# A decoder block on one core: the attention product of the folded weights in three float32r passes instead of one float32 product

## The reference

```python
x = _layernorm(x + _L0_attn_ref(x, ...))      # eight heads of eight columns
x = _layernorm(x + _L0_xattn_ref(ctx, ctx, x))
x = _layernorm(x + _L0_ffn_ref(x, ...))       # linear layer plus a chosen low-rank part
x = _layernorm(x + _L1_attn_ref(x, ...))      # codes looked up, see below
x = _layernorm(x + _L1_xattn_ref(x, ctx, ...))
x = _layernorm(x + _L1_ffn_ref(x, ...))       # ternary weights
```

```python
q, k, v = (_lin_lora(x, _dequant(codes[n], scales[n]), A[n], B[n]) for n in (0, 1, 2))
attn = (q + k + v) / 3.0
o = _lin_lora(attn, _dequant(codes[3], scales[3]), A[3], B[3])
x1 = x + o
h = silu(_lin_lora(x1, gate)) * _lin_lora(x1, up)
return x1 + _lin_lora(h, down)
```

## Time and profile before

| what | us |
|---|---|
| median of 3 runs (lowest, highest) | 634.55 (633.81, 635.37) |
| the profiled execution's own time | 634.79 |
| its span in the trace | 633.0 |
| PE busy in the span | 620.7 |
| DVE busy | 449.5 |
| ACT busy | 388.7 |
| POOL busy | 64.7 |

### The profile page before, as it was taken

How to read it: one execution, slowest core, us unless ns; L and a number is a source line. 1 busy time by engine, 2 the same in 40 slices (tenths; PEclk the granted TensorE clock), 3 DMA queues, 4 the chain that set the end, 5 groups by cost and what they waited for, 6 DMA issues and landing times.

```text
span 633.0 us, 8684 instructions
## 1 busy us (share of the span) xinstructions
PE 620.7 (98%) x3186; PEld 460.6 (73%) x3186; DVE 449.5 (71%) x718; ACT 388.7 (61%) x564; POOL 64.7 (10%) x116
## 2 busy tenths in 40 slices
PE   9999999999999999999999999999999999999996
PEld 6655555544568888878888888887777788887874
DVE  5788787557678979898987627334675777777467
ACT  2977798746677688686966136232558545667532
POOL 1032133211130000000000000001221000000012
PEclk9999999999999999999999999999999999999999
DMA  8763486302134135443630005019001133200002
GB/s 254 286 186 114 163 277 208 101 1 86 56 91 119 51 98 153 131 141 91 180 108 19 1 0 167 1 50 419 30 1 34 50 101 100 67 0 2 1 34 101
DMA packets 25777, 64.46 MB, mean 102 GB/s; under 512 B 5601, under 2 KB 10785, under 8 KB 24966
## 3 DMA queue, kind: packets, MB, share of 16 engines
q1 hardware_dynamic: 23478, 62.19, 30.6%
q10 hardware_dynamic: 2256, 1.70, 0.9%
HBM read 59.27 MB, written 4.60 MB: 101 GB/s over the span
## 4 chain that ended last, share of the span: by engine, by line
PE 80%; ACT 7%; DVE 5%; DMA 4%; issue 2%; SPq 1%; POOL 0%; POOLq 0%; DVEq 0%; ACTq 0%
PE bank L1126 19%; PE bank L1262 10%; PE bank L1114 5%; PE bank L1115 5%; PE bank L1113 5%; PE bank L965 4%; PE bank L885 4%; PE bank L689 3%; ACT line L1398 3%; DMA b_gu<-in_b_gu 2%; PE bank L995 2%; PE bank L824 2%; PE bank L1204 2%; PE bank L1205 2%; DMA codes<-in_c_qkv 1%
## 5 line engine op out<-in xcount | busy, mean ns | idle before, releaser
L1398 ACT ACTIVATE line<-line 128x1024 f32<-128x1024 f32 x87 | 91.4, 1050 | 0.1
L1113 PE MATMUL bank<-xh,wh 128*128 128x512 f32 x224 | 87.4, 390 | 0.0
L1114 PE MATMUL bank<-xl,wh 128*128 128x512 f32 x224 | 87.4, 390 | 0.0
L1115 PE MATMUL bank<-xh,wl 128*128 128x512 f32 x224 | 87.3, 390 | 0.0
L1126 PE MATMUL bank<-wh,xh 128*128 128x512 f32 x176 | 69.7, 396 | 0.2 <-DVE xl L2387 0.2
L1126 PE MATMUL bank<-wh,xl 128*128 128x512 f32 x176 | 68.6, 390 | 0.0
L2387 DVE TENSOR_TENSOR xl<-arena,xh 128x1024 fp32r<-128x1024 f32 (+1 forms) x24 | 28.3, 1179 | 35.7 <-ACT xh L1703 35.5
L1703 ACT ACTIVATE xh<-arena 128x1024 fp32r<-128x1024 f32 (+1 forms) x24 | 24.4, 1021 | 39.6 <-PE bank L1126 35.3
L1115 PEld LDWEIGHTS bank<-xh,wl 128*128 128x128 f32 x224 | 42.0, 188 | 8.8
L1113 PEld LDWEIGHTS bank<-xh,wh 128*128 128x128 f32 x224 | 42.1, 188 | 8.6
L1114 PEld LDWEIGHTS bank<-xl,wh 128*128 128x128 f32 x224 | 42.1, 188 | 8.4
(11 more groups left out here) (288 smaller groups left out, 1354.2 us busy)
## 6 DMA issues: line engine op xcount, KB each, us to landing
codes<-in_c_gu SPq DMA_DIRECT2D x14, 512.0 KB, 5.1
scales<-in_s_gu SPq DMA_DIRECT2D x28, 256.0 KB, 3.9
codes<-in_t_gu SPq DMA_DIRECT2D x8, 512.0 KB, 4.3
codes<-in_c_dn SPq DMA_DIRECT2D x7, 512.0 KB, 5.0
scales<-in_s_dn SPq DMA_DIRECT2D x14, 256.0 KB, 3.9
fold<-in_t_dn SPq DMA_DIRECT2D x1, 3584.0 KB, 15.7
codes<-in_c_qkv SPq DMA_DIRECT2D x6, 512.0 KB, 4.6
scales<-in_t_gu SPq DMA_DIRECT2D x6, 512.0 KB, 4.1
```

Of the source, the lines that this page charges most:

```text
L1113: pe.matmul(dst, wh[:, s, c:c + P], xh[:, k, cols], start=(k == 0), stop=False)
L1114: pe.matmul(dst, wh[:, s, c:c + P], xl[:, k, cols], start=False, stop=False)
L1115: last = pe.matmul(dst, wl[:, s, c:c + P], xh[:, k, cols], start=False, stop=(k == KD - 1))
L1398: nc.scalar.activation(below(slot), below(slot), ACT.Prelu, bias=bias, scale=scale, alpha=alpha).then_inc(bent, 1)
```

## The change

`attention_product` multiplies in three float32r passes. For that, ACT makes high parts of the four parts of `wsum` and of `woT` (`rows_high(j)`, two copies of 128 x 512 in each of the steps 0 to 3), and DVE subtracts them in place to get the low parts (`rows_low(j)`, two instructions in each of the same steps). One semaphore, `af_added`, counts all six instructions of a j. The high parts lie in `fold` and in `wh`. The high part of the down stack, which lay in `wh`, now lies in `m_hi`, so it is made and used up earlier: `down_stack_hi` moves from steps 2 and 3 to 0 and 1, `down_stack_low` from step 4 to 1, and the other two stacks move back, to steps 2 and 3 on ACT and to 5 and 6 on DVE. The units of the lookup, one in each step before, stand as 1, 0, 1, 0, 2, 1, 2, 1.

```diff
-PLAN = ([0] + [1] * (NT - 1), [2], [0] + [1] * 7, [1] * NT)
+PLAN = ([0] + [1] * (NT - 1), [2], [0] + [1] * 7, [1, 0, 1, 0, 2, 1, 2, 1])
...
-        ad_high = wh[:, :, :].rearrange("p s c -> p (s c)")[:, 0:FF]
+        ad_high = m_hi[:, :, :].rearrange("p k c -> p (k c)")[:, 0:FF]
+        w_hi = [fold_r[:, NF - 6 + n, :] for n in range(KD)]
+        wo_hi = [wh[:, n // 2, n % 2 * D:(n % 2 + 1) * D] for n in range(KD)]
+        w_lo, wo_lo = (arena_r[:, m_at:m_at + KD * D].rearrange("p (j c) -> p j c", j=KD) for m_at in (0, KD * D))
...
                 if n >= 2 and not o:
-                    pe.wait_ge(af_added, n)
+                    pe.wait_ge(af_added, 3 * n - 4)
...
                 if c == 0:
-                    pe.wait_ge(af_added, 2 * KD)
+                    pe.wait_ge(af_added, 6 * KD)
...
                 for j in range(KD):
-                    pe.matmul(dst[:, :], wsum[:, j, c * P:(c + 1) * P], woT[:, j, :], start=(j == 0), stop=False)
+                    pe.matmul(dst[:, :], w_hi[j][:, cols], wo_hi[j], start=(j == 0), stop=False)
+                    pe.matmul(dst[:, :], w_hi[j][:, cols], wo_lo[:, j, :], start=False, stop=False)
+                    pe.matmul(dst[:, :], w_lo[:, j, cols], wo_hi[j], start=False, stop=False)
                 pe.matmul(dst[:, c * P:(c + 1) * P], threes, ident[:, :], start=False, stop=True).then_inc(m_ps, 1)
...
+            def rows_high(j):
+
+                act.wait_ge(af_added, 6 * j + 2)
+                if j == 0:
+                    act.wait_ge(kq_ps, NT)
+                nc.scalar.activation(w_hi[j], wsum[:, j, :], ACT.Copy).then_inc(af_added, 1)
+                nc.scalar.activation(wo_hi[j], woT[:, j, :], ACT.Copy).then_inc(af_added, 1)
...
                 act.wait_ge(m_ps, c + 1)
+                if c == 0:
+                    act.wait_ge(stack_low, 1)
...
                 for u, h in half_plan(3, t, 0):
                     unit_bends(u, h)
+                if t < KD:
+                    rows_high(t)
                 if t >= 1:
                     norm_tail(2 * NT + t - 1)
                 if FIRST_M <= t < FIRST_M + KD:
                     m_high_of(t - FIRST_M)
+                if t == 0:
+                    act.wait_ge(in_lora, 16 * 4)
+                if t < 2:
+                    down_stack_hi(t)
+                elif t < 4:
+                    stack_hi_of(t - 2)
...
-                if t < 2:
-                    stack_hi_of(t)
-                elif t < 4:
-                    down_stack_hi(t - 2)
...
+            def rows_low(j):
+
+                dve.wait_ge(af_added, 6 * j + 4)
+                nc.vector.tensor_tensor(w_lo[:, j, :], wsum[:, j, :], f32(w_hi[j]), ALU.subtract).then_inc(af_added, 1)
+                nc.vector.tensor_tensor(wo_lo[:, j, :], woT[:, j, :], f32(wo_hi[j]), ALU.subtract).then_inc(af_added, 1)
...
-                if t in (1, 2):
-                    stack_low_of(t - 1)
+                if t in (NT - 3, NT - 2):
+                    stack_low_of(t - NT + 3)
                 for u, h in half_plan(3, t, 0):
                     unit_part(u, h)
-                if t == 4:
+                if t == 1:
                     down_stack_low()
+                if t < KD:
+                    rows_low(t)
```

More of the change, by code:

```diff
@@ L217, in decoder_kernel @@
         m_hi = sb("m_hi", [P, KD, D], F32R)
+        with nc.sbuf_tensor("fold_r", [P, NF, D], F32R) as fold_r:
+            pass
         fold = sb("fold", [P, NF, D])
@@ L993, in attention_product @@
                 dst = bank[4 + c % 2]
+                cols = slice(c * P, (c + 1) * P)
                 for j in range(KD):
-                    pe.matmul(dst[:, :], wsum[:, j, c * P:(c + 1) * P], woT[:, j, :], start=(j == 0), stop=False)
+                    pe.matmul(dst[:, :], w_hi[j][:, cols], wo_hi[j], start=(j == 0), stop=False)
+                    pe.matmul(dst[:, :], w_hi[j][:, cols], wo_lo[:, j, :], start=False, stop=False)
+                    pe.matmul(dst[:, :], w_lo[:, j, cols], wo_hi[j], start=False, stop=False)
                 pe.matmul(dst[:, c * P:(c + 1) * P], threes, ident[:, :], start=False, stop=True).then_inc(m_ps, 1)
@@ L2221, in add_lora @@
                 nc.vector.tensor_tensor(dst, dst, bank[4 + n % 2][:, :], ALU.add).then_inc(af_added, 1)
+            def rows_low(j):
+                dve.wait_ge(af_added, 6 * j + 4)
+                nc.vector.tensor_tensor(w_lo[:, j, :], wsum[:, j, :], f32(w_hi[j]), ALU.subtract).then_inc(af_added, 1)
+                nc.vector.tensor_tensor(wo_lo[:, j, :], woT[:, j, :], f32(wo_hi[j]), ALU.subtract).then_inc(af_added, 1)
             def stack_low_of(part):
-                dve.wait_ge(stack_hi, part + 1)
+                dve.wait_ge(stack_hi, part + 3)
                 if part == 0:
@@ L2231, in down_stack_low @@
             def down_stack_low():
-                dve.wait_ge(stack_hi, 4)
+                dve.wait_ge(stack_hi, 1)
                 nc.vector.tensor_tensor(ad_st[2 * RG:STACK, :], a_down[2 * RG:STACK, :], f32(ad_high[2 * RG:STACK, :]), ALU.subtract).then_inc(stack_low, 1)
```

## The result

The changed kernel takes **636.86 us** (median of 7 runs, 636.46 to 637.73), and the kernel before, on the same chip, 635.37 (7 runs, 633.81 to 635.77). The ratio is 1.0024, with a 95% interval of 1.0014 to 1.0034: slower by 1.5 us, within 0.3%, as forecast. The forecast had 0.6 us. The median before was 0.8 us higher in this comparison than the 634.55 on which the forecast was built, so of the 1.7 us between 635.2 and 636.86 some 0.8 belongs to the baseline and 0.9 to the forecast of the change.

What follows compares the result with a forecast made beforehand. PE, busy for 98% of the span, was taken to bound the kernel. A gain of 2.52 us and waits of 1.14, 1.0 and 1.0 gave +0.6 us on 634.55, so 635.2 us as median, range 632.5 to 637.2.

Steps and rivals of the forecast that it cites:

- my own case: Whole run: PE's saving less three waits, +0.6 us, 635.2 us as median, own range 633.9 to 636.4, chance 0.52.
- The gain: PE in `attention_product`: twelve float32r matmuls take 2.80 us instead of 3.43, so four products save 2.52 us.
- First wait: `ffn_W(4)` in step 2: PE waits for DVE's add of `ln_head(1)` to empty its bank, losing 1.14 us.
- Second wait: `attention_product(0)` in step 3: PE waits for `rows_low(3)`, losing 1.0 us.
- Third wait: `x_T(4)` at the end of step 6: PE waits for `x_low(3)`, losing 1.0 us.
- I cost them at nothing: ACT between `x_T(4)` and `x_T(5)`: four lookup activations, 4.2 us, in a gap of some 7.6 us, priced at nothing.
- The second rival: Behind `ln_head(4)` and `ln_head(5)`: POOL held up, high parts of `M` late, PE pays; 635.9 to 637.0 us, chance 0.25.
- The first rival: At the three waits: they are shorter and the gain stays; without any wait 632.0 us, chance 0.20.
- The third: Rival on the products: float32r passes don't overlap, a product takes 4.68 us, time 639.6 or above, chance 0.03.
- Passed on whole: Behind the stage: whatever PE gains or loses by 190 us is passed on whole to the run's time.

Runs made afterwards that it cites:

- low_late: Changed kernel with the down stack's low part moved on DVE from step 1 to step 3, behind `rows_low(3)`: 636.25 us, ratio 1.0006 to the kernel before.
- last_j: Changed kernel where only the last three matmuls of the first product wait for `rows_low(3)`: 635.94 us, ratio 0.9998 to the kernel before.
- flat_plan: Changed kernel with the lookup's units back to one in each step: 637.88 us, ratio 1.0036 to the kernel before.
- plan_only: Kernel before with only the new places of the lookup's units: 636.86 us (median of 11), ratio 1.0019.
- fill3: Changed kernel with lookup units 1, 0, 1, 2, 1, 1, 1, 1 and the down stack's low part in step 3: 634.0 us, ratio 0.9977 to the kernel before.
- best: `fill3` together with the edit of `last_j`, on the changed kernel: 633.14 us (median of 6), ratio 0.9962 to the kernel before.
- both: Changed kernel with the edits of `low_late` and `last_j` together: 635.25 us, ratio 0.9992 to the kernel before.
- pool_first: Changed kernel where DVE waits in step 6 for POOL's inverse deviation of tile 6 before it joins: 637.18 us (one run).

## Why the forecast was right, and what it missed

- **Faster, same or slower.** Within 0.3% was the likeliest, at 0.65, and so it came, though the interval of the ratio (1.0014 to 1.0034) reaches a little past it. 636.86 is inside the range, near its upper end. It is outside my own case's narrower range, 633.9 to 636.4; only on the old baseline, 634.55 + 1.5 = 636.05, would the measured change lie in it. The forecast's +0.6 is less than half of what was measured, and that the total still held is in part the width that I had given the rivals: a wait as large as most of the others had been left out.
- **The gain.** 2.52 forecast, 2.46 measured, 2.89 and 2.87 us for a product instead of 2.80. Right in mechanism; the part that I mis-sized is the first matmul of a group, 0.31 to 0.34 instead of 0.23. The trace of before had it: the twelve of `attention_out(1)`, from 189.26 to 192.14, take 2.88, and I had measured from the third start on, where the first distance is not in it.
- **First wait.** 1.14 forecast, 1.17 measured. It rested on an unbroken run of DVE's instructions. `low_late` shows its cause: without the down stack's low part 0.31 remain.
- **Second wait.** 1.0 forecast, 0.92 measured. `last_j` shows its cause: it is `rows_high(3)` and `rows_low(3)` behind the last sums. `flat_plan` shows that with the join back ahead of `x_low(0)` it is more, as the step said: 1.92 in the bracket instead of 0.76.
- **Third wait.** 1.0 forecast, 1.16 measured, in a sum of 10.57 us. `flat_plan` and `plan_only`, neither of which has it, show that the moved units and the earlier work are both needed for it.
- **"I cost them at nothing".** This is the step that failed. I had named ACT's cover between `x_T(4)` and `x_T(5)` as the thinnest and counted four activations against it, but not the time for which ACT stands still ahead of a `norm_tail` because POOL is late. I stopped at `x_T(5)`. The wait came one tile later, at `x_T(6)`, and cost 0.84 us of the 1.0 by which +0.6 was short of the shift, +1.64. `plan_only` and `fill3` show that it is the plan's. The trace of before had the warning:

```profile
187.63 0.81 ACT L1452 ACTIVATE x<-rbuf,rstd 128x512 f32<-128x512 f32 x1 [1.80 <-POOL rstd L1940]
...
190.84 0.68 DVE L2056 TENSOR_TENSOR xl<-bank,xh 128x512 fp32r<-128x512 f32 x1
```

  ACT already waited 1.80 us for POOL at this tile, and `x_low(5)` was over at 191.52 with `x_T(6)` starting at 192.14. Less the 0.14 from DVE to PE that is 0.5 us to spare, a third of the 1.5 at `x_T(4)`, which I did cost.
- **The second rival** had the mechanism right and the place wrong. As it said, POOL's first instruction took over 1 us behind `ln_head(4)`, 1.12 from 174.86; the other two took 0.57 and 0.62 and ended at 177.34, so that `norm_tail(20)` started at 177.38. That end is 4.9 us after `lora_out(4)` (172.40), where I had 5.9. But the low part of `M` at 179.20 had no wait for it, and the price at that place was nothing. Behind `ln_head(5)` DVE waited 0.24 us for `m_high_of(3)`, and `x_T(5)` lost nothing. The same thing behind `ln_head(6)` was paid for. That 636.86 lies within this rival's price, 635.9 to 637.0, is luck as far as its own two places go. The rule of the Trainium skill (page "SBUF — State Buffer", section "Who interferes with whom") was cited there, and the trace agrees: 1.10, 1.59 and 1.34 us beside a two-input instruction of DVE, 0.23, 0.57 and 0.27 without. What I did wrong with it was to weigh it as a rival at two places rather than to lay it over each `ln_head` of the new order, as I did with DVE's sums.
- **The first rival** (the gain stays) fell by its own sign: `attention_out(1)` starts at 191.31 and not at 187. That is 2.05 later than 189.26, more than the 1 us given; 1.27 of it already lies ahead of `lora_T(0)`, and counted from there it is 0.78. Its time, 632.0, is nearly that of `best` (633.14 against 635.61 is -2.47), which has the passes and only one short wait. **The third** fell by the product's 2.87 us.
- **Passed on whole.** The last gate-stack row that I compared lies 166.69 us behind `lora_T(0)` before. There the shifts are +1.76 after the change, +2.15 `flat_plan`, +1.29 `plan_only`, +0.83 `low_late`, +0.85 `last_j`, -0.34 `both`, +2.29 `pool_first`, -1.23 `fill3`, -2.26 `best`, against +1.64, +1.91, +1.08, +0.77, +0.63, -0.26, +2.31, -1.24 and -2.29 at 72 us. So it was right for losses and for gains, within 0.24 us.

What stays open is small. The wait of 0.24 us at `ffn_W(4)`, which the two subtractions of `rows_low(1)` would explain, was not taken away by any run. Why a float32r group's first matmul is slower behind a transpose or a wait than behind `ffn_W`, no run shows.

## What to carry to other kernels

Work that is taken from the engine that bounds the time and given to idle ones is paid for where it stands, not by its amount: here 9 us of new work on ACT and DVE, with the lookup moved about it, cost 4.1 us at four places, and 0.3 us at one once more of it lay in a gap and a wait asked only for what the next instruction reads. Lay out the new order of every engine in the loop against the times at which its results are due, for every step, with the small engine too: three instructions on 128 x 1 values took 4 us because of what stood beside them. And count from an instruction that both kernels have just ahead of the change, since here the spans alone hold over 1 us of scatter.

## What was unexpected of the hardware

- A chain of three tiny POOL instructions can be caught by each of the following instructions of DVE in turn: 0.23 + 0.57 + 0.27 = 1.07 us of work became 4.03 (1.10 + 1.59 + 1.34), as each in turn met a two-input instruction of 1.2 us. Once caught, the second took 2.8 times its own length and the third 5 times.
- The first matmul of a float32r product takes 0.34 us to the next start where eleven others take 0.23 (158.80 to 159.14 against 159.14 to 159.37). Where no wait is named it takes 0.31 (164.13 to 164.44), and in `last_j`, right behind `ffn_W(5)`, nothing extra shows.
- The bracket of a wait says less than the loss: 0.90, 0.76 and 0.69 in the brackets were 1.16, 0.92 and 0.84 from start to start.
